# A transformer block on one core: two of the eight expert choices moved from VectorE to GpSimd

## What is computed

```python
h = _layernorm(x) * (1 + cb) + sb
q = (h @ Wq).reshape(b, t, 2, H, RET // 2)             # H = 4 heads
sim = jnp.einsum('btphn,hkpn->pbthk', q, keys)          # 2 x 64 keys per head
sc, ix = jax.lax.top_k(sim, 8)
all_sc = sx[..., :, None] + sy[..., None, :]
scores, pk = jax.lax.top_k(all_sc, 8)                   # 8 of 512 experts
w = jnp.einsum('btd,bthkd->bthk', h, down_embed[idx])
w = silu(w) * softmax(scores)
experts = jnp.einsum('bthk,bthkd->btd', w, up_embed[idx])
```

## Time and profile before

| what | value |
|---|---|
| median of 3 runs | 1450.23 us (1448.07 to 1450.8) |
| profiled execution, first to last instruction (the only time that its page gives) | 1448.7 us, 39838 instructions |
| TensorE clock granted | 0.995 of full |
| VectorE busy | 1289.4 us, 89% |
| ScalarE busy | 1270.9 us, 88% |
| GpSimd busy | 1052.9 us, 73% |

### The profile page before, as it was taken

The page is one execution under the profiler, slowest core; times in us unless marked ns, Lnnn a source line. Parts: engine busy times, 40 slices in busy tenths (PEclk is TensorE's granted clock), DMA queues, the critical chain, the costliest instruction groups (busy, mean ns, idle before and its releaser), DMA issues.

```text
span 1448.7 us, 39838 instructions
## 1 busy us (share of the span) xinstructions
PE 1399.7 (97%) x11491; PEld 1161.5 (80%) x11491; DVE 1289.4 (89%) x5345; ACT 1270.9 (88%) x4212; POOL 1052.9 (73%) x1221
## 2 busy tenths in 40 slices
PE   6899999999999999999999999999999999999998
PEld 4678788888788888788888788888788888788887
DVE  5589999999999999999999999999999999999977
ACT  6788988898988898988898988898988898988885
POOL 2048787778787777787777787787787777777760
PEclk9999999999999999999999999999999999999999
DMA  4000000000000000000000000000000000000000
GB/s 132 16 14 21 15 10 20 20 16 20 13 11 20 20 16 20 14 10 20 20 16 20 13 11 20 20 16 20 15 9 20 20 16 20 14 10 24 10 14 10
DMA packets 51041, 27.74 MB, mean 19 GB/s; under 512 B 10336, under 2 KB 50208, under 8 KB 51008
## 3 DMA queue, kind: packets, MB, share of 16 engines
q1 hardware_dynamic: 50768, 26.91, 7.1%
q10 hardware_dynamic: 240, 0.43, 0.1%
HBM read 23.02 MB, written 4.31 MB: 19 GB/s over the span
## 4 chain that ended last, share of the span: by engine, by line
PE 81%; ACT 14%; issue 3%; DVE 1%; DMA 0%; SPq 0%; POOL 0%; ACTq 0%; DVEq 0%; POOLq 0%
PE pW L1457 10%; PE pS L1527 9%; PE pW L1540 9%; PE pW L1568 8%; PE pW L1459 8%; PE pW L1458 8%; PE pS L1517 7%; PE pS L1513 6%; PE pW L1613 4%; PE pW L1610 4%; ACT pT L652 4%; ACT pS L660 4%; PE pW L1544 3%; PE pW L1601 2%; ACT h L750 2%
## 5 line engine op out<-in xcount | busy, mean ns | idle before, releaser
L660 ACT ACTIVATE pS<-pS,nmx 128x128 f32<-128x128 f32 (+1 forms) x1024 | 389.4, 433 | 33.2 <-DVE nmx L1085 33.2
L1085 DVE CUSTOM_DVE_ANT_0 pS<-pS,mask 128x128 f32<-128x128 f32 (+1 forms) x1024 | 331.8, 390 | 27.2 <-PE pS L1517 22.7
L504 POOL TENSOR_TENSOR fexp<-fexp,fsum 128x512 f32<-128x512 f32 x240 | 299.9, 1284 | 76.6 <-DVE fexp L1214 76.6
L652 ACT COPY pT<-pS 128x768 f32<-128x768 f32 x256 | 216.1, 844 | 42.2 <-PE pS L1527 40.4
L495 POOL TENSOR_TENSOR fsum<-ex 128x512 f32<-128x512 f32 x248 | 250.6, 1047 | 0.0
L1527 PE MATMUL pS<-ident,p_sb 128*128 128x128 f32 x1536 | 216.3, 277 | 6.1 <-DVE p_sb L1105 4.2
L1105 DVE TENSOR_TENSOR p_sb<-pS,coef 128x256 f32<-128x256 f32 (+2 forms) x512 | 210.5, 453 | 8.9
L1527 PEld LDWEIGHTS pS<-ident,p_sb 128*128 128x128 f32 x1536 | 173.7, 141 | 37.3 <-issue 18.9
L660 ACT ACTIVATION_READ_ACCUMULATOR pS<-pS,nmx 128x1 f32 x1024 | 193.7, 189 | 0.0
L642 ACT COPY qk<-pW 128x512 f32<-128x512 f32 x256 | 162.2, 634 | 4.6 <-PE pW L1459 1.1
L1540 PE MATMUL pW<-pT,v 128*64 128x256 f32 x1024 | 165.9, 402 | 0.3 <-ACT pT L652 0.2
(11 more groups left out here) (211 smaller groups left out, 3696.1 us busy)
## 6 DMA issues: line engine op xcount, KB each, us to landing
x_in<-in_L_attn_tokens SPq DMA_DIRECT2D x32, 128.0 KB, 2.1
x_res<-in_L_attn_tokens SPq DMA_DIRECT2D x32, 128.0 KB, 3.0
modB<-mods_dram SPq DMA_DIRECT2D x32, 128.0 KB, 2.9
modA<-mods_dram SPq DMA_DIRECT2D x31, 128.0 KB, 3.1
out<-yo SPq DMA_DIRECT2D x31, 128.0 KB, 1.9
modC<-mods_dram SPq DMA_DIRECT2D x32, 64.0 KB, 3.2
fsum<-in_L_attn_Wkv SPq DMA_DIRECT2D x1, 512.0 KB, 6.0
w_out<-in_L_attn_Wout SPq DMA_DIRECT2D x1, 512.0 KB, 7.2
```

Of the source, the lines that this page charges most:

```text
L504: ins = nc.gpsimd.tensor_tensor(fexp[:, k, h, :], fexp[:, k, h, :], fsum[:, k, h].rearrange("p i j -> p (i j)"), ALU.mult)
L652: nc.scalar.copy(pT[:, p % 2], pS[:, p % 2, :, 0:SW]).then_inc(S(pT_ready), 1)
L660: ins = nc.scalar.activation(ps, ps, ACT.Exp, bias=nmx[:, p % 2, h, k:k + 1], scale=-1.0, accum_out=den(p)[:, h, k:k + 1])
L1085: ins = nc.vector.tensor_tensor_reduce(out=ps, in0=ps, in1=mask[:, (1 - k) * P:2 * P], scale=-1.0, scalar=LARGEST, op0=ALU.add, op1=ALU.mi ...
```

## The change

The two choices of `choose(1, 1)` (heads 2 and 3 of the second block of rows) leave DVE's program. POOL makes them in a new function `choose_rest`, called between `rstd2` and `weigh(1)`, with the same operation and operands. It waits for the second block's products and for `rz`, and counts up a new semaphore, `masks_pool`, on which `weigh(1)` waits besides `masks_ready`; that one is now counted up after `choose(0, 1)` and after `choose(1, 0)`. The unrolled last steps, which choose in another way, keep their work.

Besides, DVE's functions are cut so that each holds the instructions between two waits: `normalise` into `invert`, `coefficients` and `normalise`, `ln2_stats` into `gate_attention`, `add_residual`, `stats2` and `aggregate2`, `ln1_stats` and `ln1_modulate` into `stats1`, `aggregate1`, `center1`, `scale1`, `shift1` and `square1`, `shift` into `row_largest`, `shift` and `shift_top`, `thresholds` into `top_candidates`, `sum_top` and `invert_top`, `finish` into `gate_output` and `finish`. The helper `link`, which put a wait behind an instruction, is gone; the wait stands at the head of the next function. The calls stand in the same order. The waits for `modA`, for `x_res` and, in `normalise(0)`, for the value banks move behind the first instruction of their old function.

The diff, cut to the choices and to three of the cuts in DVE's program:

```diff
-        ln1_chain, attn_chain = ev("ln1_chain", LN1_LINKS), ev("attn_chain", ATTN_LINKS)
+        ln1_chain, inverse_ready = ev("ln1_chain", LN1_LINKS), ev("inverse_ready", NP)
...
-        masks_ready = ev("masks_ready", TB)
+        masks_ready, masks_pool = ev("masks_ready", TB), ev("masks_pool", 1)
...
+                def choose_rest():
+                    if w.live(-2):
+                        pool.wait_ge(S(f_ready[1]), at(f_ready[1], g, 1))
+                        pool.wait_ge(S(rz_ready), at(rz_ready, g, 1))
+                        apart()
+                        for h in range(RH // 2, RH):
+                            ins = nc.gpsimd.tensor_scalar(fexp[:, 1, h, :], fsum[:, 1, h].rearrange("p i j -> p (i j)"),
+                                                          top8[:, 1, h, TK - 1:TK], rz[:, 1, h:h + 1], ALU.is_ge, ALU.mult)
+                        ins.then_inc(S(masks_pool), 1)
+
                 def weigh(k):
                     if w.live(-2):
                         pool.wait_ge(S(masks_ready), at(masks_ready, g, k + 1))
+                        if k == 1:
+                            pool.wait_ge(S(masks_pool), at(masks_pool, g, 1))
...
                 fold(0)
                 rstd2()
+                choose_rest()
                 weigh(1)
...
                 def choose(k, half):
...
-                        if half == 1:
+                        if k + half == 1:
                             ins.then_inc(S(masks_ready), 1)
...
-                normalise(2)
-                ln2_stats()
+                invert(2)
+                coefficients(2)
+                normalise(2)
+                gate_attention()
+                add_residual()
+                stats2()
+                aggregate2()
                 gate_product(2)
-                choose(1, 1)
+                invert(3)
+                coefficients(3)
                 normalise(3)
...
-            def modulate1(b):
+            def center1(b):
                 dve.wait_ge(S(rstd1_out), at(rstd1_out, b, 1))
+                for k in range(TB):
+                    ins = nc.vector.tensor_scalar(h1[:, k, :], x_in[:, k, :], mv1[:, k, 0:1], rs1[:, k:k + 1], ALU.subtract, ALU.mult)
+                ins.then_inc(S(ln1_chain), 1)
+
+            def scale1(b):
                 if not isinstance(b, int) or b > 0:
                     dve.wait_ge(S(modA_loaded), at(modA_loaded, b - 1, 16))
-                for k in range(TB):
-                    ins = nc.vector.tensor_scalar(h1[:, k, :], x_in[:, k, :], mv1[:, k, 0:1], rs1[:, k:k + 1], ALU.subtract, ALU.mult)
-                link(ins, ln1_chain, b)
+                dve.wait_ge(S(ln1_chain), at(ln1_chain, b, 2))
```

More of the change, by code:

```diff
@@ L1087, in row_max, with invert, coefficients @@
                         ins.then_inc(S(max_ready), 1)
-                def normalise(p):
+                def invert(p):
+                    if w.live(0):
+                        dve.wait_ge(S(exp_ready), at(exp_ready, i, p + 1))
+                        nc.vector.reciprocal(den(p), den(p)).then_inc(S(inverse_ready), 1)
+                def coefficients(p):
                     if w.live(0):
@@ L1098, in normalise @@
                         ins.then_inc(S(coef_ready), 1)
+                def normalise(p):
+                    if w.live(0):
                         dve.wait_ge(S(coef_ready), at(coef_ready, i, p + 1))
[L1100 to L1101 removed]
                         mine = slice(0, 1) if p in SHARED else slice(0, 2)
@@ L1134, in low_part, with ln1, gate_attention @@
                         w.release(nc.vector.tensor_tensor(parts[1][:, :], w.bank(name)[:, 0:N], parts[0][:, :], ALU.subtract), name)
-                def ln1_stats():
+                def ln1(part):
                     if w.live(1) and not first:
[L1138 to L1144, removed]
+                        part(i + 1)
+                def gate_attention():
                     if w.has("op"):
-                        dve.wait_ge(S(res_loaded), at(res_loaded, f, 16))
                         dve.wait_ge(S(modB_loaded), at(modB_loaded, f, 16))
@@ L1269, in body @@
                     row_max(1)
+                    invert(0)
+                    coefficients(0)
                     normalise(0)
+                    invert(1)
+                    coefficients(1)
                     normalise(1)
@@ L1278, in body @@
                     row_max(5)
+                    invert(4)
+                    coefficients(4)
                     normalise(4)
+                    invert(5)
+                    coefficients(5)
                     normalise(5)
-                    ln1_modulate()
+                    ln1(center1)
+                    ln1(scale1)
+                    ln1(shift1)
+                    ln1(square1)
                     row_max(6)
@@ L1284, in body @@
                     low_part(xT_high, xT, "xT")
+                    invert(6)
+                    coefficients(6)
                     normalise(6)
+                    invert(7)
+                    coefficients(7)
                     normalise(7)
@@ L1383, in body @@
                 bias_product(2)
+                invert(2)
+                coefficients(2)
                 normalise(2)
-                ln2_stats()
+                gate_attention()
+                add_residual()
+                stats2()
+                aggregate2()
                 gate_product(2)
-                choose(1, 1)
+                invert(3)
+                coefficients(3)
                 normalise(3)
-                ln1_stats()
+                ln1(stats1)
+                ln1(aggregate1)
                 bias_product(3)
@@ L1394, in body @@
                 low_part(h2T_high, h2T, "hT")
+                invert(4)
+                coefficients(4)
                 normalise(4)
+                row_largest(0)
                 shift(0)
+                invert(5)
+                coefficients(5)
                 normalise(5)
-                ln1_modulate()
+                ln1(center1)
+                ln1(scale1)
+                ln1(shift1)
+                ln1(square1)
+                row_largest(1)
                 shift(1)
+                shift_top()
                 row_max(6)
@@ L1402, in body @@
                 low_part(xT_high, xT, "xT")
+                invert(6)
+                coefficients(6)
                 normalise(6)
+                gate_output()
                 finish()
                 bias_product(0)
+                invert(7)
+                coefficients(7)
                 normalise(7)
```

118 lines of the change are left out of this document (75 added, 43 removed).

## The result

The changed kernel takes 1575.68 us (median of 4 runs, 1571.27 to 1578.24), the kernel before 1449.15 beside it (4 runs): the ratio is 1.0875, 95% interval 1.0849 to 1.09. It is slower, as forecast, but by 126.5 us and not by 26, far above the upper end of the range, 1502 us. The profiled execution has a span of 1573.6 us.

What follows compares the result with a forecast made beforehand. It took TensorE, busy 97% of the span, as the bound, with POOL's delay holding DVE's layer norm: span 1448.7 us, plus 29 x 0.9 = 26, plus 1.5, gives 1476 us; range 1449 to 1502 us for 8 in 10.

Steps and rivals of the forecast that it cites:

- Off DVE: `choose(1, 1)` leaves DVE; the gain ends in DVE's idle time before `bias_product(3)`, 0 us for the path.
- The gain on `rstd2`: On POOL, `rstd2` no longer runs beside `choose(1, 1)` and ends 0.30 us earlier.
- Onto POOL: Two `tensor_scalar` of 128x512 with two pointers, taken at 0.85 us each, make POOL 1.5 us later from `weigh(1)` on.
- POOL and DVE get in each other's way: POOL's addition L514 would lie over the start of DVE's layer norm (L987) and hold it, 0.9 us per step.
- The price for being late: POOL 1.5 us later costs DVE's layer norm 0.9 us in each of 29 steps, +26 us.
- The chain to TensorE: DVE's layer norm, `rms1`, `fold(1)` and L524 reach TensorE's load with less than 0.1 us to spare.
- Where TensorE waits: Sign: TensorE's loads at L1601 wait for POOL's `d_t`, 0.9 us in each step.
- POOL's wait for `ms`: Sign: POOL's idle time before L538 falls from 2.58 to about 2 us, not to 1.1.
- Neither is late: Despite POOL's delay, `rstd1` is ready for DVE and `wsum` for ScalarE's `total(1)` in time.
- No change: Rival: DVE's layer norm is not held, POOL's 1.5 us vanish in its wait; about 1450 us, chance 0.13.
- faster: Rival: DVE's free 1.0 us shortens TensorE's wait for ScalarE's copies, at most 13 us, 1437 us; chance 0.09.
- Slow compare: Rival: POOL's instruction costs as much as a two-input one or more; 1502 us and above, chance 0.10.

Runs made afterwards that it cites:

- the idle measurement: Kernel before, with ten forms of POOL instruction, four times each, after its last output is stored, all other engines idle; 1514.0 us in one execution.
- the run with the clock held up: Changed kernel with 16 more matmuls of 128x256, which nothing reads, on TensorE ahead of `transpose_x`; 1534.06 us, ratio 1.0582.

## Why the prediction was wrong in size

The direction, the place and the first mechanism, the held layer norm, were right. Two terms of the sum were not: the price of POOL's instruction, and TensorE's clock, which the sum put at nothing. Of the 100 us that the forecast lacked, 59 are the longer hold (85 instead of 26) and 42 the clock. Point by point:

- **Off DVE, 0 us: right.** The wait of `bias_product(3)` grew as forecast, from 1.40 to 1.83 us before L1145.
- **The gain on `rstd2`: right.** L547 and L549 of before (L559 and L561 now) take 0.24 and 0.72 us in the step of the changed kernel, and from the end of the statistics to L506 it is 1.77 us (641.24 to 643.01), 0.25 less than it was to `weigh(1)`.
- **Onto POOL, the step that failed:** "I take the cast with two pointers, 0.61 + 0.24 = 0.85 us each". Measured 2.07, and even its bound "about 1.4 us" was too low. The reasoning went from the cast and the compare-and-fill to the form with two pointers, as if all of POOL's one-input instructions were alike. By the idle measurement they are not: 0.61 us for the copy, 1.5 to 2.1 us for nearly all others. The two-input instruction, 1284 ns, was no ceiling. The Trainium skill (GPSIMD Engine Reference, section 4.1) calls GpSimd's one-input work "roughly line-rate"; the runs agree for the copy and for multiply and add by constants (0.61 and 0.62 us), not for the choice, at 3.4 ns per column.
- **POOL and DVE get in each other's way: right, and the open point is settled.** The prediction had no row in which L987 was held. Now its median is 1257 ns against 341, and it ends with POOL's additions. L1004, with two SBUF inputs, is held as well, 1508 against 426; in the run with one choice, 2.13 us later, it still took 425 in the median.
- **The price for being late: right.** The forecast had 0.9 us of loss at 1.5 us; between the runs with two copies (1.01, 0.45) and two early choices (1.59, 0.96) a straight line gives 0.88. At the true 4.05 us the same mechanism takes 2.98 by the timeline and 2.94 by the run with the clock held up, 85 us in all. Only the 1.5 was wrong.
- **TensorE's clock: missing from the sum, the second step that failed.** The prediction gave no reason for leaving it out; in its rows TensorE waits 0.44 us once per step, and the mean clock is 0.995. Measured: 1.43 us per step, 41.6 in all. With 85.2 for the hold, by the groups, that makes 126.8, against 126.5 measured.
- **The chain to TensorE: right in effect.** The rows leave 0.12 us between the end of L524 (656.23) and the load (656.35), not "less than 0.1"; the table of runs shows that the hold comes through to the time in full.
- **Where TensorE waits: half right.** The sign named was L1601 (now L1706), 0.9 us. Here the wait stands mostly one group earlier, at `transpose_x`, 2.15 us for `xr`, and 0.67 at L1706. Both hang on `rms1`, as the prediction had it.
- **POOL's wait for `ms`:** forecast about 2 us, measured 1.45. That is near 2.58 - 4.05 + 2.98 = 1.51: the wait of before, less POOL's own delay, plus the delay that it handed to DVE.
- **"Neither is late":** `total(1)` now waits for `wsum`, 46.4 us over 30 waits on ScalarE. The statement holds at 1.5 us, since the run with two early choices, 1.59 us later, has no such wait in its table; it does not at 4.05.
- **The rivals.** No change and faster are out: the change is slower, and DVE's relief bought nothing in any run. Slow compare was nearest: 1502 us at 1.38 each and 6 us for each further 0.1 gives 1543 at 2.07, and with the clock held up it is 1534. Its name was wrong, for comparing costs no more than multiplying, and it too lacked the clock.

## What to carry to other kernels

A wait on an engine is room only if what it waits for does not depend on that engine's own work: POOL's 2.58 us would be free by start times alone, but POOL's additions hold the very layer norm that it waited for. An instruction whose form is in no row should be measured by itself, in idle time at the end of the kernel, before it is moved: a factor of 3.4 between a copy and a `tensor_scalar` of the same tile decided this case. And where a wait stops TensorE itself, look at the granted clock behind it: the slow matmuls after it added another half of what the wait cost.

## What the hardware showed that was not expected

- On POOL, 128x512 fp32, with all other engines idle: copy 0.61 us, multiply and add by constants 0.62, one multiplication by a constant 1.49, one operation by a pointer 1.56, comparison and multiplication by constants 1.93, by pointers 2.08. A product of the tile with itself takes 1.04, less than one multiplication by a constant.
- Waits of 2.15 and 0.67 us, with two matmuls between them, went with a clock of 0.62 in the mean of the 4.5 us from the end of the first; waits of 0.51 and 0.67 us, in a step of the run with one choice, left it at 1.00. Matmuls that nothing reads, put into the wait, kept it at 1.00.
